# Picks dropped from the last five steps of layer 0, and other pacing waits for GpSimd, in a two-layer graph kernel

## The reference

```
e_feat = concat(x[src], x[dst], edge_attr)              # layer 0, per edge
v = relu(e_feat @ W1 + b1) @ W2 + b2
x = layernorm(x + maximum(segment_max(v, dst), x))

xs, y = h[src], h[dst]                                  # layer 1, per edge (h is the new x)
msg = einsum(w_comp[etype], xs, weight)
a = tanh(relu(sum((xs @ A1_w.T + A1_b) * (y @ A2_w.T + A2_b + rel_emb[etype])) / sqrt(32)))
nei = segment_sum(a * msg, dst)
x = layernorm(x + relu(where(in_degree > 0, nei + h[src[last_edge]] @ self_loop_weight, 0)))
```

## Time and profile before

| | us |
|---|---|
| median of 3 runs | 4362.16 |
| lowest and highest | 4360.83, 4362.19 |
| the profiled execution itself | 4359.81 |
| its span, first to last instruction | 4358.0 |
| PE busy in it | 3805.1 (87%) |
| GpSimd busy | 3216.5 (74%) |
| VectorE busy | 3057.2 (70%) |
| ScalarE busy | 904.1 (21%) |

### The profile page before, as it was taken

One profiled execution on the slowest core, in us unless ns is written; L12 is line 12 of the kernel. 1 busy time (PEld: TensorE's weight loads), 2 busy tenths in 40 slices (PEclk: granted clock), 3 DMA queues, 4 the chain that ended last, 5 costly groups with the idle time before them and its releaser, 6 DMA issues.

```text
span 4358.0 us, 75158 instructions
## 1 busy us (share of the span) xinstructions
PE 3805.1 (87%) x22557; PEld 1726.1 (40%) x22780; DVE 3057.2 (70%) x4872; ACT 904.1 (21%) x1615; POOL 3216.5 (74%) x3349
## 2 busy tenths in 40 slices
PE   7889999999999999931079999999999999999941
PEld 3444545545545545421033333333333333333311
DVE  7846666666666666536068888888888888888844
ACT  4411111111111111110022222222222222222211
POOL 7777777777777777767777777777777777777745
PEclk9999999999999999965589999999999999999975
DMA  8123333333333333324055555555555555555511
GB/s 339 29 81 103 98 100 91 100 98 92 98 98 94 95 97 98 100 49 76 16 129 139 140 139 138 141 143 138 136 143 140 136 142 141 138 138 143 139 47 32
DMA packets 411463, 493.91 MB, mean 113 GB/s; under 512 B 165619, under 2 KB 315136, under 8 KB 409184
## 3 DMA queue, kind: packets, MB, share of 16 engines
q1 hardware_dynamic: 274368, 277.48, 25.0%
q0 software_dynamic: 107040, 133.47, 13.3%
q10 hardware_dynamic: 29952, 81.80, 5.0%
HBM read 345.64 MB, written 146.76 MB: 113 GB/s over the span
## 4 chain that ended last, share of the span: by engine, by line
PE 35%; DMA 9%; issue 4%; POOL 1%; DVE 1%; ACT 0%; POOLq 0%; DVEq 0%; ACTq 0%
PE psum L1487 8%; PE psum L1422 8%; DMA xg<-h_dram,src_idx 7%; PE psum L1413 6%; PE psum L1469 5%; DMA last_rows<-sum_rows,last_i 2%; PE psum L1496 2%; PE psum L1314 1%; PE psum L1430 1%; PE psum L1451 1%; POOL xg L640 1%; PE psum L1473 1%; PE psum L1439 1%; PE psum L1304 1%; DVE late L1171 0%
## 5 line engine op out<-in xcount | busy, mean ns | idle before, releaser
L640 POOL DMA_INDIRECT xg<-h_dram,src_idx x1564 | 1507.3, 964 | 487.0 <-DMA xg<-h_dram,src_idx 352.6
L640 POOL DMA_INDIRECT xg<-in_x_dram,src_idx x1387 | 1324.3, 955 | 451.4 <-DMA xg<-in_x_dram,src_idx 304.6
L1171 DVE TENSOR_TENSOR late<-late,psum 128x512 f32<-128x512 f32 x1664 | 1082.8, 682 | 285.1 <-PE psum L1413 214.2
L1328 PE MATMUL psum<-early,late 128*128 128x448 bf16 x5817 | 1155.2, 354 | 9.7 <-DVE late L984 7.6
L1328 PEld LDWEIGHTS psum<-early,late 128*128 128x128 bf16 x5817 | 554.9, 98 | 643.7 <-issue 124.1
L1413 PE MATMUL psum<-comp,sel 128*128 128x512 bf16 x1458 | 524.0, 383 | 14.0 <-DVE late L1171 8.1
L1422 PE MATMUL psum<-late,basis 128*32 128x512 f32 x3328 | 445.2, 607 | 0.1
L1487 PE MATMUL psum<-x,late 128*128 128x448 bf16 x1400 | 396.5, 353 | 0.0
L984 DVE TENSOR_TENSOR late<-psum,lane_hot 128x448 f32<-128x448 f32 x277 | 173.1, 625 | 316.9 <-PE psum L1328 273.0
L1092 DVE TENSOR_TENSOR_SCAN scan<-fresh,scan,psum 128x512 f32<-128x512 bf16 x103 | 131.8, 1279 | 306.7 <-PE psum L1374 306.6
L965 DVE TENSOR_SCALAR late<-late,class_id 128x384 bf16<-128x384 f32 (+2 forms) x728 | 335.6, 529 | 0.0
(11 more groups left out here) (151 smaller groups left out, 4102.4 us busy)
## 6 DMA issues: line engine op xcount, KB each, us to landing
sp_in<-spread SPq DMA_DIRECT2D x208, 256.0 KB, 6.1
late<-type_dram SPq DMA_DIRECT2D x104, 512.0 KB, 8.4
sum_rows<-early ACTq DMA_DIRECT2D x104, 512.0 KB
spread<-late SPq DMA_DIRECT2D x16, 1664.0 KB, 39.0
ea<-in_edge_t SPq DMA_DIRECT2D x104, 256.0 KB, 3.5
keep<-keep_dram SPq DMA_DIRECT2D x832, 32.0 KB
max_rows<-out ACTq DMA_DIRECT2D x104, 256.0 KB, 2.1
xg<-h_dram,src_idx POOLq DMA_INDIRECT x1564
```

Source lines behind the costliest of these rows:

```text
L640: pool.indirect_dma_start(out=out, out_offset=None, in_=table, in_offset=bass.IndirectOffsetOnAxis(ap=index, axis=0), engine_sem=pool_issu ...
L1171: dve.tensor_tensor(prod[:, n % G_BUFS, :], x4[:, s.slot(2), g, :], bank[C_BANK[n]][:, :], ALU.mult).then_inc(prod_ready, 1)
L1328: last_ = pe.matmul(hot_bank[tile_slot(s, t)], class_hot[s.slot(2)][:, HOT - hot_tiles(s) + t, c, :], x_parts[:, c, q, :], start=c == 0 an ...
```

## The change

Five edits. `hot_count` is 0 instead of 1 in the last five steps, so their 16 tiles are all gathered, and PE and VectorE leave these picks out (`pe_picks` in place of `hot`). `build_hot` still builds one tile's matrices there, since layer 1 uses them. `after_thirds` becomes `after_work`: a step of PE counts 26 units of work and 21 more for each tile that it picks, the gathers are laid over the sum of the units, with 16 calls added to their number, and a call waits for the third of a step that lies 120 units before its share. In the search the waits of the gathers begin at call 40 instead of 28, and a scatter waits for a column that is 12 lower.

```diff
-SLACK0 = 3
+STEP_WORK = 26
+PICK_WORK = PARTS * CLASSES
+SLACK0 = 120

 def hot_count(n):
-    return HOTS[n % len(HOTS)] if n < FEW_HOT else 1
+    return HOTS[n % len(HOTS)] if n < FEW_HOT else 0

+        def pe_picks(s):
+            return hot(s) and hot_tiles(s) > 0

-            def after_thirds(n, k):
+            step_work = [STEP_WORK + PICK_WORK * (hot_count(n + 2) if n + 2 >= PRE and n + 2 < STEPS else 0) for n in range(STEPS)]
+
+            def after_work(n, k):
                 if k % BURST:
                     return
-                s, third = divmod((calls_before[n - PRE] + k) * 3 * STEPS // calls_before[-1] - SLACK0, 3)
-                if s < 0:
+                work = (calls_before[n - PRE] + k) * sum(step_work) // (calls_before[-1] + SLOTS) - SLACK0
+                s = 0
+                while work >= step_work[s]:
+                    work -= step_work[s]
+                    s += 1
+                if work < 0:
                     return
+                third = 3 * work // step_work[s]
                 if third == 0:
                     pool.wait_ge(x_turned[0], s + 1)
                 elif third == 1:
...
-                        after_search(calls[0], 28, 0)
+                        after_search(calls[0], 40, 0)
...
-                after_search(k, 0, 72)
+                after_search(k, 0, 60)
...
-                tiles = slice(HOT - hot_tiles(s), HOT)
+                tiles = slice(HOT - max(hot_tiles(s), 1), HOT)
...
-                if hot(n):
+                if pe_picks(n):
```

More of the change, by code:

```diff
@@ L675, in gathers0 @@
                     if s.at >= PRE:
-                        after_thirds(s.at, k)
+                        after_work(s.at, k)
                     else:
-                        after_search(calls[0], 28, 0)
+                        after_search(calls[0], 40, 0)
                     gather(xg0[:, s.slot(PRE), k, :], t["x_dram"], src_idx[:, s.slot(PRE), k:k + 1],
```

## The result

| | before | after |
|---|---|---|
| median of six runs, us | 4360.88 | 4380.49 |
| lowest and highest, us | 4358.81, 4362.19 | 4375.64, 4383.22 |
| span of the profiled execution, us | 4358.0 | 4381.4 |
| GpSimd: last gather of layer 0 | 1903.32 | 1888.74 |
| first fetch of results | 1918.99 | 1906.76 |

The ratio after/before is 1.0045, with a 95% interval of 1.0033 to 1.0057. The change makes the kernel some 20 us **slower**, where 14.5 us less were forecast.

The account below looks back on a forecast made before the run. GpSimd's gathers were taken to bound the kernel, the last one setting layer 0's end. Terms -21.2 + 6.3 = -14.9, by the pitch -14.5 (taken): 4362.16 - 14.5 = 4347.7 us, range 4343.5 to 4353.

Parts of the forecast that it names:

- GpSimd's pauses: Layer 0: GpSimd's waits for PE in front of gathers, lost to the old pacing, would go, saving 21.2 us.
- The new waits cost nothing: Layer 0: the new pacing's waits cost 0, bound 4 us; the smallest slack is 3.9 us, in step 12.
- rival 2: Layer 0, early steps: the new waits stop GpSimd, 4 to 6 us lost, about 4352.5 us; chance 0.05.
- Five more gathers cost 6.3 us: Steps 99 to 103 of layer 0: 16 gathers instead of 15, +6.3 us on GpSimd before the last gather.
- Step 103 at 1891.2: End of layer 0: PE starts step 103 at 1891.2, 2.4 us after the last gather at 1888.8.
- PE's saving is needed: End of layer 0: dropped picks save PE some 20 us; without that, step 103 starts only at 1899.5.
- Rival 1: End of layer 0: PE becomes the bound, steps stay between 12.9 and 14.3 us, gain 6.2, 4356.0 us; chance 0.05.
- The cold tail, rival 3: PE's steps 97 to 103 all run at 1.2 GHz, 15.6 us a step, 4370.0 us; chance 0.03.
- Rival 4: Layer 0: buffers or index loads stop GpSimd where pacing did; only the added gathers count, 4368.5 us; chance 0.03.
- The node stage as before: Stage between layers 0 and 1, 257 us: GpSimd's 197 DMAs set it, so an earlier start shifts it whole.
- The step that failed: After layer 0: the whole gain, taken as 14.5 us, was to pass through the node stage and layer 1.
- layer 1 as long as before: Layer 1, a sign to check in the profile after: its length unchanged, 1564 gathers in 1989 us.

Follow-up runs that it names:

- the padded kernels: The kernel after with 20 or 225 small VectorE memsets added ahead of layer 1's loop: 4350.84 us, and 4348.96 us in a single run.

## Why the prediction was wrong

- **GpSimd's pauses (21.2 us) go**: right, none is left.
- **The new waits cost nothing, rival 2 does not come**: right; no wait for PE over 0.3 us after 281.
- **Five more gathers cost 6.3 us, last gather at 1888.8**: right, 1888.74; with the old pacing 1908.71, 5.4 later than before. Five undisturbed profiled executions with the full change and the new pacing (one of them with the scan replaced) had it between 1888.34 and 1893.13.
- **Step 103 at 1891.2, first fetch at 1904.5**: 1892.12 and 1906.76. From the last gather to the first fetch 18.0 us went by where the sum took 15.7 over from before. Of these 2.3 us, 1.0 lie before step 103 starts (3.4 us behind the last gather, not 2.4) and 1.4 in the step: its PE work took 8.99 us at a granted clock of 0.73, behind a wait of 9.45, where it took 7.60 at 0.88.
- **PE's saving is needed**: right for the stage, and of no use for the kernel. With the picks kept, step 103 started at 1897.59 and the first fetch came at 1910.29, 3.5 us later than in the kernel after. The five executions with the full change spread from 1906.55 to 1911.35, however, so the size of this gain is not settled. Rival 1's mechanism holds in that kernel. Yet it took 4348.02 us, no more than the padded kernels with the picks dropped (4350.84 and 4348.96).
- **The cold tail, rival 3**: steps 97 to 100 took 9.13 us each, at a granted clock of 0.98; the tail of 15.6 us a step did not come. The price that the prediction held to be paid already was a little larger: steps 102 and 103 ran at 0.72 and 0.73, and it is the 1.4 us above. Rival 4 did not come.
- **The node stage as before**: right within 1 us, 257.1 and 258.0 us.
- **The step that failed**: "In layer 1 ... an earlier start shifts all of it. I take the whole amount as passed on", with "layer 1 as long as before" as its sign. It took 34.7 us more, and the sum had no term for it. I had priced the removed picks by the time of VectorE's and PE's work that goes, at nothing since other work hides it. A removed instruction has a second effect that no row of the trace before shows: all code behind it moves. Here VectorE's loop moved by 20 instructions over an edge, paused 22 times, and the pauses and the catching up let some 34 more gathers start inside a scan, at up to 0.94 us each. Nothing in the rows of before could have given the size: the same pauses cost 16.3 us in the kernel before with 236 memsets.

Added up from the start of layer 1: forecast -14.5, found -11.4 there, +34.7 in layer 1, and the stage behind it equal (153.8 and 153.9 us), which is the 23.4 of the spans. The place of the loop is shown as the cause, by the kernels in which nothing but small instructions of VectorE is added (1490 against 1510 in the kernel after, 1510 against 1746 in the kernel before; the same twenty behind the loop change nothing), and so is the part of the scan. That the pauses are instruction fetches is seen directly, in a packet of the instruction queue inside each of the 22. That the edge lies between blocks of 256 rests on six places of the loop and on the section of the Trainium skill named above, not on a direct view.

## What to carry to other kernels

When an edit adds or removes instructions ahead of a loop, count them on each engine, waits included, and compare the page's row on instruction fetches: 64 packets against 174 told at once that a loop had begun to fetch at each turn, although its code was equal. They do not tell the price, which was 34.7 us in the kernel after, 16.3 in the kernel before and nothing without the scan. Twenty small instructions ahead of the loop, placed in idle time, took the fetches away, and the same twenty behind it did not. Here it was a loop of 289 instructions; loops of other lengths were not run. And an engine that is never late by the idle times may still lose time inside its instructions: compare the mean of one (964 against 987 ns), not the waits alone.

## What the runs showed of the hardware

**A gather held by a scan.** I took the starts of the gathers against those of the 104 scans L1198 of the kernel after. In 37 cases the gather began 0.14 to 0.33 us behind the scan, and it took 1.70 to 1.89 us. At 0.65 behind it took 1.38, at 0.92 it took 1.11, from 1.09 on 0.94 to 0.95; and in the 43 cases that began up to 0.2 ahead of the scan also 0.94 to 0.95. So a gather begun between 0.14 and 1.05 us behind the start of the scan ends 2.03 us behind it (1.97 for the first scan, which is 0.06 shorter), 0.75 behind the scan's end, as if it stood until the scan is over; one begun before it is not touched. The scan with one of its inputs in PSUM (L1083), equally long, does nothing of the kind: 84 gathers of layer 1 began 0.14 to 1.05 us behind one and took 0.96 at most. Beside the one shown above, from 2556.82, the gather begun 0.63 behind it took 0.94:

```profile
2557.45 0.94 POOL L646 DMA_INDIRECT xg<-h_dram,src_idx  x1 [0.30 <-PE psum L1425]
```

The Trainium skill, "SBUF — State Buffer", section "Who interferes with whom", has a VectorE instruction with two SBUF inputs contend only with GpSimd instructions that read SBUF, and infers that making descriptors needs the write side. These rows differ from the inference: a gather is held by such a scan. The same section says that issue order decides who blocks. The trace agrees for the gather begun first, which is not held; but the scans begun up to 0.2 us behind a gather are not held by it either, all 43 took 1.27 to 1.28 us.

**A smaller one of the same kind.** Beside `one_hot` (128x2048, one SBUF input) many gathers take 1.1 to 1.3 us, and those begun up to 0.4 us behind its start up to 1.47, in both kernels:

```profile
2564.57 1.27 POOL L646 DMA_INDIRECT xg<-h_dram,src_idx  x1 [0.30 <-DMA xg<-h_dram,src_idx]
```

```profile
2564.97 0.75 DVE L1159 TENSOR_SCALAR late<-late,row_id 128x2048 bf16<-128x2048 bf16 x1
```

50 gathers of layer 1 are between 1.20 and 1.32 us before, 67 after, and 22 in the kernel after without the scan. What the gathers beside `one_hot` took beyond 0.945 us each adds up to 28.6 us before and 31.0 after, so this effect is in both kernels and has 2.4 us in the loss.
